# A graph network layer's first stage: four products per pair on quarters of the array, one pair of banks, later tables

## What is computed

```python
h = silu(edge_scalars @ Wfc1);  w0, w1, w2, w3 = split(h @ Wfc2)      # 64, 64, 32, 32
e0 = (x0 @ Wl1_0)[src];  e1 = (x1 . Wl1_1)[src];  sh0, sh1 = edge_attr[:, :1], edge_attr[:, 1:]
mid0 = w0 * e0 * sh0;            mid1 = w3 * sum_m(e1 * sh1)
mid2 = w1 * e0 (x) sh1;          mid3 = w2 * e1 * sh0
n = segment_mean(mid, dst);      scal = [n0, n1];  vec = [n2, n3]
conv = [scal @ Wl2_s, vec . Wl2_v];  alpha = scal @ Wa
out = layernorm(x + x @ Wsc + alpha * conv)
```

## Time and profile before

| | |
|---|---|
| median of three executions | 903.74 us |
| the profiled execution, its span | 900.12 us, 898.4 us |
| busy share of the span: PE, DVE, POOL, ACT | 94%, 90%, 79%, 70% |
| TensorE's granted clock, mean | 0.992 |
| HBM read and written | 119.66 MB, 64.95 MB |
| edge stage, last message on VectorE | 552.2 us |

### The profile page before, as it was taken

How to read it: one execution, slowest core, us unless ns; L and a number is a source line. 1 busy time by engine, 2 the same in 40 slices (tenths; PEclk the granted TensorE clock), 3 DMA queues, 4 the chain that set the end, 5 groups by cost and what they waited for, 6 DMA issues and landing times.

```text
span 898.4 us, 33828 instructions
## 1 busy us (share of the span) xinstructions
PE 845.2 (94%) x11276; PEld 713.2 (79%) x11276; DVE 810.1 (90%) x2797; ACT 628.3 (70%) x1961; POOL 713.5 (79%) x804
## 2 busy tenths in 40 slices
PE   2999899999999999999999988999999999999994
PEld 1788788888887887888888877888888888888884
DVE  3798899999998999999999987999999999999997
ACT  1555455555555555565565554999999999999998
POOL 6777777777777776777777711999999999999995
PEclk9999999999999999999999999999999999999998
DMA  6455544544557676557764412899999999999994
GB/s 184 122 169 168 153 134 137 139 129 130 133 145 151 187 209 182 174 163 204 210 179 133 130 69 101 249 307 311 317 299 309 332 332 305 311 319 307 316 310 159
DMA packets 87544, 186.85 MB, mean 208 GB/s; under 512 B 17646, under 2 KB 48138, under 8 KB 87371
## 3 DMA queue, kind: packets, MB, share of 16 engines
q1 hardware_dynamic: 50715, 93.00, 31.9%
q0 software_dynamic: 18944, 35.81, 18.1%
q10 hardware_dynamic: 17712, 55.87, 18.1%
HBM read 119.66 MB, written 64.95 MB: 205 GB/s over the span
## 4 chain that ended last, share of the span: by engine, by line
PE 50%; DVE 14%; SPq 12%; issue 12%; DMA 6%; POOL 4%; ACT 2%; DVEq 0%; ACTq 0%; POOLq 0%
PE ps L831 9%; SPq L467 9%; PE ps L772 7%; PE ps L751 6%; PE ps L732 5%; PE ps L769 5%; PE ps L738 5%; DVE mid L1024 4%; PE ps L817 3%; SPq L457 3%; DVE z L1042 3%; PE ps L714 3%; PE ps L847 3%; PE ps L712 3%; POOL gat L620 2%
## 5 line engine op out<-in xcount | busy, mean ns | idle before, releaser
L620 POOL DMA_INDIRECT gat<-turned,srcs x196 | 192.2, 981 | 65.6 <-issue 61.2
L620 POOL DMA_INDIRECT gat<-spread,srcs x196 | 187.7, 958 | 62.4 <-issue 59.1
L901 ACT ACTIVATE te<-ps 128x512 f32<-128x512 f32 x196 | 106.4, 595 | 123.7 <-PE ps L738 120.8
L831 PE MATMUL ps<-win,eas 60*128 60x162 f32 x2352 | 190.0, 306 | 1.1 <-DVE eas L1367 0.7
L772 PE MATMUL ps<-wy,mid 128*128 128x161 f32 x784 | 182.3, 314 | 0.0
L831 PEld LDWEIGHTS ps<-win,eas 60*128 60x128 f32 x2352 | 165.6, 186 | 18.0 <-DVE eas L1367 11.0
L1048 DVE SCALAR_TENSOR_TENSOR msg<-ps,sha,z 128x161 f32<-128x161 f32 x392 | 151.0, 385 | 13.9
L686 POOL TENSOR_TENSOR gat<-eas,gat 128x640 f32<-128x640 f32 x98 | 152.0, 1551 | 10.9 <-ACT eas L946 10.5
L769 PE MATMUL ps<-wy,mid 128*128 128x97 f32 x784 | 141.6, 262 | 0.2 <-DVE mid L1024 0.2
L1024 DVE TENSOR_TENSOR mid<-ps,te 128x512 f32<-128x512 f32 x196 | 133.3, 680 | 3.3 <-PE ps L751 3.3
L924 ACT ACTIVATE te<-gat,shift,rstd 128x160 f32<-128x160 f32 x292 | 131.8, 533 | 2.7 <-DVE shift L1314 1.3
(11 more groups left out here) (110 smaller groups left out, 1501.1 us busy)
## 6 DMA issues: line engine op xcount, KB each, us to landing
win<-rows SPq DMA_DIRECT2D x392, 114.6 KB, 4.0
rows<-msg SPq DMA_DIRECT2D x98, 326.0 KB
out<-te ACTq DMA_DIRECT2D x47, 640.0 KB, 6.6
xin<-x_g ACTq DMA_DIRECT2D x76, 322.0 KB, 5.7
kept_x<-x_g SPq DMA_DIRECT2D x16, 322.0 KB
gat<-turned,srcs POOLq DMA_INDIRECT x196
gat<-spread,srcs POOLq DMA_INDIRECT x196
eas<-ea_t SPq DMA_DIRECT2D x7, 384.0 KB, 3.8
```

What stands on the lines that cost most here:

```text
L620: pool.indirect_dma_start(out=gat[:, slot, first:first + of.shape[1]], out_offset=None, in_=of, in_offset=bass.IndirectOffsetOnAxis(ap=src ...
L831: last = nc.tensor.matmul(agg_ps[b1][:, 2 * h + k, 0:SW], hot[side(h), b1, k, c, :], win[side(h), (RING * i + b - 1) % WIN_RING, k, c, 0:S ...
L901: nc.scalar.activation(e_sb[:, t, :], e_ps[:, t], ACT.Copy).then_inc(e_out[t], 1)
```

## The change

A message row becomes five chunks of 33 columns (32 numbers and one single: count, label, gate), 165 instead of 163 numbers. Each product runs as matmuls on quarters of the array: 64 rows of `mid` (half of the sum) and 64 edges each. Those of rows 0 to 63 write bank 6, those of rows 64 to 127 bank 7, at chunks of 33 columns that lie 66 apart. Both pairs use these two banks in turn, so that `combine` waits for the messages of the pair before it. `weigh` is split: `find_e` no longer waits for messages. ScalarE empties a pair in one instruction (132 numbers), VectorE makes the vector part in two for a pair; the sum is one per tile as before, 165 wide. The label is written by an operation with two operands (the larger of a number and itself) into z. Of GpSimd's tables two stay at step 14, the others go behind its last gather; the pads and labels of the windows are set by VectorE, and the passes over the moved tables run behind VectorE's last message.

```diff
-                if p == 1:
+                if p == 0:
                     pe.wait_ge(heads_out, 2)
+                    pe.wait_ge(wy_ready, 12)
                 for t in range(2):
                     pe.wait_ge(mid_ready[t], q + 1)
-                    if k == 0:
-                        pe.wait_ge(e_out[t], min(q + 2, NS))
-                    if q >= 1:
-                        pe.wait_ge(msg_ready[t], p - 1)
-                    nc.tensor.matmul(y[:, t, 0:W_Y1 - W_YA], mid[:, q % 2, t, 0, k, :],
-                                     wy[:, 0:W_Y1 - W_YA], start=True, stop=True)
...
+                    if p >= 1:
+                        pe.wait_ge(msg_ready[t], p)
+                low, high = slice(0, HALF), slice(HALF, P)
+                made = ((0, 0, low, W_V, y_at(0, -4)[:, :, 0:MUL1]),
+                        (0, 0, high, W_YA, y_at(0, 1, 2)),
+                        (0, 1, low, W_Y1, y_at(0, -3, 3)),
+                        (0, 1, high, W_Y1, y_at(0, 0, 2, 3)),
+                        (1, 0, low, W_YA, y_at(1, -2, 2)),
+                        (1, 0, high, W_V, y_at(1, 3)[:, :, 0:MUL1]),
+                        (1, 1, low, W_Y1B, y_at(1, -4, 2)),
+                        (1, 1, high, W_Y1B, y_at(1, 0, 3)))
+                for t, c, half, w, y in made:
+                    width = y.shape[1] * y.shape[2]
+                    for edges in (low, high):
+                        last = nc.tensor.matmul(
+                            y[edges], mid[half, q % 2, t, c, k, edges],
+                            wy[half, w - W_YA:w - W_YA + width].rearrange(
+                                "p (j w) -> p j w", j=y.shape[1]), start=True, stop=True)
+                last.then_inc(y_ready, 1)
             def step(d):
+                if alive(d, 3):
+                    combine(d - 3, 0)
                 if alive(d, 0):
                     first_layer(d)
-                for k in range(2):
-                    if alive(d, 0):
+                    for k in range(2):
                         turn(d, k)
-                    if alive(d, 3):
-                        combine(d - 3, k)
+                if alive(d, 3):
+                    combine(d - 3, 1)
                 if alive(d, 1):
-                    weigh(d - 1)
+                    find_e(d - 1)
+                    find_w(d - 1)
...
+                nc.vector.tensor_tensor(z[:, :, :, LABEL], now, now, ALU.max
+                                        ).then_inc(label_ready, 1)
...
-            edge_steps(step, {CONSTANTS: more_constants, STARTS - 6: find_windows})
+            edge_steps(step, {CONSTANTS: more_constants, STARTS - 6: find_windows,
+                              NS - 1: last_constants})
...
+            take_iotas(6, columns, g_spare)
+            lower_labels()
+            take_labels()
+            dve.wait_ge(iotas_ready, 5)
```

More of the change, by code:

```diff
@@ L234, in gnn_kernel, with y_at @@
         w_ps = ps[:, 4:6, :]
[L235 to L237 removed]
+        heads_ps = ps[:, 6:8, 0:T // 2]
+        wrong_ps = ps[0:1, 6, T // 2:T // 2 + 1]
+        y_ps = ps[:, 6:8, :].rearrange("p c e -> p (c e)")
+        def y_at(t, j, count=1, every=1):
+            flat = y_ps
+            lanes = flat[:, 512 - YB:512 + YB].rearrange("p (j t w) -> p j t w", t=2, w=CHUNK)
+            return lanes[:, j + 4:j + 4 + (count - 1) * every + 1:every, t, :]
         g_ps = ps[:, 7, 0:SW]
@@ L1028, in label, with finish @@
             def label(q):
-                half = slice(q % 2 * QUAD, (q % 2 + 1) * QUAD)
-                if q >= 2:
+                if q >= 1:
+                    for t in range(2):
+                        dve.wait_ge(msg_ready[t], 2 * q)
+                now = dsts[:, QUAD * q:QUAD * (q + 1)].rearrange("p (k t) -> p k t", t=2)
+                nc.vector.tensor_tensor(z[:, :, :, LABEL], now, now, ALU.max
+                                        ).then_inc(label_ready, 1)
+            def finish(q, k):
+                p, ring = 2 * q + k, q % SHA_RING
+                pair = slice(2 * k, 2 * k + 2)
+                flat = y_ps
+                first, other = 512 - 4 * LANES, 512 + 3 * LANES + CHUNK
+                v = flat[:, first:first + other - first + MUL1]
+                dve.wait_ge(zc_ready, p + 1)
+                if p >= 2:
+                    for t in range(2):
+                        dve.wait_ge(msg_ready[t], p - 1)
+                spread = sha[:, ring, pair, :].rearrange("p t m -> p (t m)")
+                nc.vector.tensor_tensor(
+                    z[:, k, :, M_A:M_S].rearrange("p t (j w) -> p t j w", j=2)[:, :, :, 0:MUL1],
+                    two_of(v, other - first, MUL1).unsqueeze(2).broadcast_to([P, 2, 2, MUL1]),
+                    two_of(spread[:, 1:], 5, 2).unsqueeze(3).broadcast_to([P, 2, 2, MUL1]),
+                    ALU.mult).then_inc(zb_ready, 1)
+                nc.vector.tensor_tensor(
+                    z[:, k, :, M_B:M_B + MUL1],
+                    two_of(v, other - first, MUL1),
+                    two_of(spread[:, 3:], 2, 1).broadcast_to([P, 2, MUL1]),
+                    ALU.mult).then_inc(zb_ready, 1)
+                if k == 0 and q >= 2:
@@ L1059, in step @@
                 if alive(d, 2):
-                    multiply(d - 2, 1)
+                    for t in range(2):
+                        multiply(d - 2, t)
                 if alive(d, 3):
@@ L1438, in pack_weights @@
         rows = slice(s * FC_H, (s + 1) * FC_H)
-        w[rows, W_W:W_W + P] = Wfc2[:, 0:P]
+        for c in range(2):
+            made = W_W + (c + 1 - s) % 2 * MUL0
+            w[rows, made:made + MUL0] = Wfc2[:, c * MUL0:(c + 1) * MUL0]
         col = W_W + P
@@ L1517 @@
         "dst_rows": rows(dst, EP + P, NP - 1),
-        "sh_t": tiles(rows(sh, EP)),
+        "sh_t": sh_t.reshape(P, -1),
         "ea_t": np.ascontiguousarray(
```

249 lines of the change are left out of this document (132 added, 117 removed).

## The result

| | before | changed |
|---|---|---|
| median (range) | 904.65 us (903.16 to 909.32) | 922.56 us (916.83 to 924.98) |
| ratio, 95% interval | | 1.0186 [1.0137, 1.0235] |
| the profiled execution's span | 898.4 us | 923.2 us |
| products of a pair, start to start | 0.99 us | 0.54 us |
| step where nothing disturbs it | 5.22 to 5.23 us (63 steps of 97 below 5.245) | 5.13 us (35 of 97 below 5.16) |

The kernel became slower, by 1.9%, with an interval clear of 1. The operations came out close to the prices forecast for them, the undisturbed ("quiet") step too, and yet the stage of steps grew by 9.65 us.

A forecast was written before the change was run, and what follows sets the result against it. TensorE was taken as the bound (5.24 us per quad), GpSimd and VectorE close below. Steps -14.1, tables -3.4, `find_windows` +0.5, label -1.9, node stage +1.5, passes +1.2 sum to -16.2: 888 us, range 878 to 904.

The forecast's parts named there:

- Of 98 steps I count 94 ... 94 x (5.24 - 5.09) = -14.1: Edge stage: 94 steps, without the four of two stalls, each shorten from 5.24 to 5.09 us, 14.1 us gained.
- the loop I had laid out: Edge stage, one pair of banks: TensorE, ScalarE and VectorE wait on each other in a closed loop of 5.09 us per quad.
- C: TensorE's products of one pair, twice in the loop: 0.99 us falls to 0.57; break-even at 0.65.
- Rival 1: The products' quarters don't get that short, as chunked writes or starts cost more: 931 us at 0.80, 967 at 0.99; chance 0.15.
- Tables: GpSimd's tables at step 14: four of six iotas, a mask and the fills leave, gaining 3.4 of 3.9 us lost.
- Label: Label write behind the last gather: with two operands it may start while GpSimd multiplies; half of 3.75 us gained, -1.9.
- Passes: Passes moved behind VectorE's last message, for which the node stage waits: +1.2 us.
- Node stage: Line 831 has 164 columns instead of 162: +1.5 us, 2.2 at most over 98 groups.
- Rival 2: GpSimd's gathers hold the edge-stage step at 5.15 to 5.20 us: 893 to 898 us; chance 0.18.
- Rival 4: Gaps of 0.4 us per quad cost TensorE its clock; five to seven falls give 907 to 915 us; chance 0.04.
- The slower side: Chance that the changed kernel is slower: 0.15, made of 0.13 from rival 1 and 0.02 from rival 4.
- The range: Forecast total of 878 to 904 us; above by rival 2 and the small end of rival 1, leaving out most of rival 1.

The follow-up runs named there:

- the two kernels that had none there: Changed kernel with GpSimd's first node-stage multiplication held until the last pair but one has its messages: 915.16 us; changed kernel with the starts' store cut into four: 921.2 us.

## Why the prediction was wrong

**The step that failed** is "Of 98 steps I count 94 ... 94 x (5.24 - 5.09) = -14.1". The step it names is real: 5.13 measured. But only 35 of 97 steps have it. The sum took 5.24, a typical step of before, and gave every step the gain of an undisturbed one, while the loop I had laid out had no slack left: each engine in it waits for the one ahead, so a disturbance adds most of its length. Before, VectorE had 0.26 to spare per quad, and an extra row of 0.54 cost 0.23; now it costs 0.42. In place of -14.1 the steps outside tables and label changed by +12.9. What the runs show of that: extra rows, which two pairs of banks swallowed again (steps 15 to 31, +2.4); a program of nearly twice the passes, for which the sum has no term and which comes late (step 47 +4.7, step 52 +1.5); extra rows and the clock together (step 59 +2.0). The rest, the first three steps (+1.4) and many losses of 0.1 to 0.7 us, was not traced to causes. Giving the loop slack (two pairs of banks) brought the tolerance back and took the gain with it.

**C, the term I feared for**, was right: 0.54 against 0.57. Rival 1 does not hold. By the Trainium skill, "PSUM — Partial Sum Buffer", section Specifications (TRN2), non-contiguous access slows matmuls significantly. These chunks of 33 columns, 66 apart, do not show it, and the measurement decides. ScalarE 0.28 (0.29), VectorE's pair 1.16 (1.15). So the size of the loop was right to 0.04 us.

**The drain was not in the sum at all**: +5.0. The text costs the new wait inside the pipeline, where features and weights lie between two products, and never walks through the last two quads, where nothing does. Giving the first pairs of these their own banks took 3.0 of it back; of the rest, TensorE's clock explains a part that no run isolates.

**Tables** -3.4, measured -3.7: right. **Label** -1.9, measured +0.4 in steps 91 to 96: the cause was wrong, since the copy's form makes no difference here and GpSimd's multiplications do; with these held back the stall is gone. **Passes** +1.2, measured +2.3: the two rows over `g_label` took 0.55 and 1.09 us, where the sum had 0.35 each; moving these and the pass over `g_spare` away gave 2.2 back. **Node stage** +1.5: the median group grew by 0.001 us, 0.1 us over all; the rest of its change is as large between executions of unchanged code.

**Rival 2** fell: TensorE waits for the messages 94 times, and one of GpSimd's four pauses is above 0.30. **Rival 4** came true in part. Its premise was that the clock falls only behind idle times above 2 us. In the trace before they were 2.36 and 2.21 us (and it fell once more near the end of the program); in the changed kernel the granted clock also falls to its lower level behind idle times of 1.55 (step 59), 1.89 (step 93) and 1.77 us (step 96), and in the drain, where the waits of 1.7 us leave it at 0.64. What a fall cost can be read at step 59 alone: 1.4 us against the two kernels that had none there. **The slower side** came, then, from a case that no rival held: a loop that is short when quiet and long when disturbed, with disturbances that the change itself adds. The range, up to 904, had no room for it.

## What to carry to other kernels

Before counting a shorter step n times, read the distribution of steps in the trace: if a new wait closes the loop, each disturbance that the old slack swallowed (extra rows, small stores, late gathers) becomes time, and the median step says little. Walk a closed loop through its last iterations too, where its cover is gone. And count instructions, not only columns: with many small products a burst of tiny DMA packets left TensorE waiting, where it cost kernels with the shorter program 1 to 3 us.

## What the runs showed of the hardware

- 512 stores of 4 bytes raise another queue's time per packet from 0.13 to 0.52 us for some 6 us; 256 at a time do so just as well (0.82 us, step 47 9.53), four of 512 bytes do not (0.11).
- With nearly twice the passes, the instruction queue taken for TensorE's has a 16 KB packet every 7.2 us, and where one came late beside the small packets the step grew by 4 to 8 us (step 47, 9.53 to 12.80 instead of 5.1). In the changed kernel's stall the rows of the matmuls end 4 us before their semaphore rises.
- TensorE's granted clock fell to its lower level behind idle times of 1.55, 1.77 and 1.89 us.
- A pair's products on halves (64 x 128) take 1.07 us, as long as their 16 weight loads (1.00); on quarters they take 0.54, while the 32 loads take 0.63.
- Beside GpSimd's multiplications a VectorE product of two SBUF tiles takes 1.28 us instead of 0.56, and a row of 128 x 4 numbers 0.74 instead of 0.15, as a copy or with two operands.
- A product that writes chunks of 33 columns, 66 apart, was not seen to take longer than its columns would in one row: 0.54 us for a pair, against 0.48 to 0.59 worked out in the prediction from products that write one run of columns.
